# Feed-forward sums: six additions on GpSimd before four TensorE products, and the normalisation on ScalarE

## The chip, the core and the metric

One core of a Trainium2 chip runs the whole program. The engines named here are TensorE (PE in the rows; its weight loads are PEld), VectorE (DVE), ScalarE (ACT), GpSimd (POOL) and the queue that issues DMAs (SP). The metric is the device time of one execution in microseconds. The kernel before takes 1882.07 us, the median of three runs (1881.39 to 1882.36).

## The reference

A transformer block over `x` of 4 x 2048 tokens with 256 channels:

```python
xn = _layernorm(x)
x = x + attention(xn) + ffn(xn)

def ffn(x):                       # W_fc 1024 x 256, W_proj 256 x 1024, both made ternary
    h = jnp.einsum('btd,hd->bth', x, absmean(W_fc))
    h = jax.nn.gelu(h, approximate=False)
    h = layernorm(h, ln_w, ln_b)  # over the 1024 hidden channels
    return jnp.einsum('bth,dh->btd', h, absmean(W_proj))
```

The layernorm inside the feed-forward needs, for each token, the sum of the 1024 values of `gelu(h)` and the sum of their squares. The attention part (16 heads of 16 channels, causal, 2048 tokens) is left as it is by this change.

## The kernel before

The program has three stages with a barrier of all engines between them. The weights are prepared in the first 41 us. The second stage, `project_and_feed_forward`, runs to about 492 us. Attention takes the rest. The change is in the second stage alone.

That stage goes over 8192 tokens in 16 turns (`ch`) of 512 tokens (`CH`). Each turn normalises 4 tiles of 128 tokens (`SUB`), transposes them, and makes three things: queries and keys (lines 884, 821, 729 to 751), values (916, 843) and the feed-forward with its residual (`R`). Each engine's program is written out by hand as a loop, in a fixed order; semaphores alone tie the engines to one another.

TensorE in a turn: the eight blocks of hidden channels (line 904, `hc` 0 to 7, between them the query and key products), the values, `sum_strips` (line 875), `down_projection` for tiles 0 and 1 (line 866), the transposes of the next turn's tokens (line 859), `down_projection` 2 and 3, and `hidden_means` (line 891). ScalarE takes each hidden block out of PSUM with Gelu into `g[:, hc, 0]` (line 831), writes the high half `gh` in fp16 (834) and the square into `g[:, hc, 1]` (836). VectorE makes the low half `gl` from `g` and `gh` (line 722, `low_g`), and a down projection may start only when all eight `gl` are there (`gl_ready`).

The sums over hidden channels are made by TensorE: `strip` is a matrix with ones, and each of 16 products of 128x32 with 128x512 in fp32 adds one block, or its square, into one of four strips of 32 rows of PSUM. Each fp32 product of this form has two records in the trace, so a turn shows 32. ScalarE copies the strips out (line 825), and `hidden_means` turns them into per-token means. VectorE then reads the means (783, `fst`), subtracts them (785), waits for GpSimd's reciprocal square root (`frs`, line 659), and writes `R` (798) from `ft` and `xc`.

GpSimd in a turn makes `rstd` for the next turn's tokens (659), adds a constant row to the tokens (664, `xc`, 128x1024 in fp32) and makes `frs`. VectorE makes the statistics of the next turn's tokens (693, 697, 700), the shift `nmr` (704) and the normalised tokens `xn` (708).

Of the kernel before, what the change touches and what calls it, by code (L numbers as in the profile page):

```python
# [7 lines left out]
ALU = mybir.AluOpType  # L8
# [3 lines left out]
P = 128  # L12
# [4 lines left out]
HC = HID // P  # L17
# [519 lines left out]
def project_and_feed_forward(nc, io, w, scr):  # L537

    with ExitStack() as ctx:
        def sb(name, shape, dt=fp32):  # L540
            return ctx.enter_context(nc.sbuf_tensor(name, shape, dt))
# [18 lines left out]
        gl = sb("gl", [P, HC, CH], fp16)  # L560
        strips = sb("strips", [P, CH])
        fst = sb("fst", [P, SUB, 2])
        fmm = sb("fmm", [P, SUB])
# [25 lines left out]
        gh_ready = sem("gh_ready")  # L589
        g2_ready = sem("g2_ready")  # L590
        gl_ready = sem("gl_ready")
        strips_summed = sem("strips_summed")
# [7 lines left out]
        hidden_bank = [bank[i] for i in (6, 7)]  # L600
        strip_bank = bank[4]
        block = ctx.enter_context(nc.Block())
# [5 lines left out]
        qk_v = [scr[m].rearrange("a b (h e) t -> a b h e t", e=DH) for m in ("Q", "K")]  # L608
        STORES = 2 * 3 * PARTS

        @block.sync
# [45 lines left out]
        def _(pool):  # L657
# [3 lines left out]
            def add_constant(par, loaded):  # L661
# [3 lines left out]
                                   in1=w["CB"][:, None, :].to_broadcast([P, SUB, C]), op=ALU.add).then_inc(xc_ready, 1)  # L665

            add_constant(0, 16)
            def body(i2, par, last):
                ch = i2 * 2 + par
                if not last:  # L670
                    pool.wait_ge(stats_ready, ch + 2)
                    rsqrt(rstd, ve).then_inc(rstd_ready, 1)
                pool.wait_ge(R_ready, ch + 1)
                if not last:
                    add_constant(1 - par, i2 * 16 + 16 + 16 * par)
                pool.wait_ge(fvar_ready, ch + 1)
                rsqrt(frs, fve).then_inc(frs_ready, 1)
# [8 lines left out]
        def _(dve):  # L686
            me = Steps(dve, steps, 13)
            spare = dve.alloc_register("spare_of_dve")
# [12 lines left out]

            def normalise(x, count):
                dve.wait_ge(rstd_ready, count)
                me.done(dve.scalar_tensor_tensor(out=nmr[:, :], in0=mv[:, :, 0], scalar=-1.0, in1=rstd[:, :],
                                                 op0=ALU.mult, op1=ALU.mult))
                me.wait()
                for s in range(SUB):
                    i = dve.tensor_scalar(xn[:, s, :], x[:, s, :], rstd[:, s:s + 1], nmr[:, s:s + 1],
                                          ALU.mult, ALU.add)
                i.then_inc(xn_ready, 1)  # L710

# [43 lines left out]
            def body(i2, par, last):  # L755
# [9 lines left out]
                if not last:  # L765
                    dve.wait_ge(xT_in_psum, ch * 2 + 2)
                    normalise(X[1 - par], ch + 2)
                low_g(ch, 5)
# [42 lines left out]
        def _(act):  # L811
# [5 lines left out]
            def high(m, ch):  # L817
# [3 lines left out]
                act.activation(part[2 * m][:, 0, :], bank[2 * m][:, :], ACT.Copy, scale=w["qscale"][:, 0:1]).then_inc(high_ready, 1)  # L821

            def strips_evac(ch):
                act.wait_ge(strips_summed, ch + 1)
                act.activation(strips[:, :], strip_bank[:, :], ACT.Copy).then_inc(strips_ready, 1)

            def body(ch, last):
                for hc in range(HC + 1):
# [12 lines left out]
                for k in range(2):  # L841
                    act.wait_ge(v_ready, ch * 2 + k + 1)
                    act.activation(Vs[:, 2 * k:2 * k + 2, :], hidden_bank[k][:, :].rearrange("p (s c) -> p s c", s=2),
                                   ACT.Copy, scale=w["pall"][:, 2:3]).then_inc(v_read, 1)
                strips_evac(ch)
                if not last:
                    xT_evac(ch + 1)

            with act.Fori(0, NCH - 1) as ch:
                body(ch, False)  # L850
            body(NCH - 1, True)

        @block.tensor
        def _(pe):
# [14 lines left out]
            def sum_strips(ch):  # L869

                pe.wait_ge(g2_ready, ch * HC + HC)
                for k in range(2):
                    for hc in range(HC):
                        q = hc % 4
                        i = pe.matmul(strip_bank[STRIP * q:STRIP * (q + 1), :], lhsT=w["strip"][:, k, :, :].rearrange("p a k -> p (a k)"),
                                      rhs=g[:, hc, k, :], start=hc + 4 * k < 4, stop=hc + 4 * k >= 8, tile_position=(0, STRIP * q))
                i.then_inc(strips_summed, 1)
# [19 lines left out]
            def body(ch, last):  # L897
# [13 lines left out]
                for k in range(2):  # L911
# [6 lines left out]
                    i.then_inc(v_ready, 1)  # L918
                sum_strips(ch)
                pe.wait_ge(gl_ready, ch * HC + HC)  # L920
                down_projection(ch, 0)
                down_projection(ch, 1)
                pe.wait_ge(v_read, ch * 2 + 2)
                pe.wait_ge(strips_ready, ch + 1)
                if not last:
                    transposes(ch + 1)
                down_projection(ch, 2)
                down_projection(ch, 3)
                for s in range(SUB):
                    hidden_means(s)  # L930
# [958 lines left out]
```

## Time and profile before

| | us |
|---|---|
| time, median of three runs | 1882.07 |
| time of the profiled execution | 1882.02 |
| its span, first to last instruction | 1880.3 |
| TensorE busy | 1818.9 |
| VectorE busy | 1671.0 |
| ScalarE busy | 1590.6 |
| GpSimd busy | 535.9 |

The busy times are sums over the whole span, in which the stage of the change is about a quarter. A turn is read from the timelines further down. A row such as `x4` in a timeline merges neighbouring instructions of one line, and its time runs from the first one's start to the last one's end. Instructions of one engine overlap a little at their ends, so what an instruction costs its engine is read from start to start.

### The profile page before, as it was taken

To read this page: it belongs to the slowest core of one execution; us is meant where nothing else is said; L and a number is where in the kernel's file an instruction comes from. 1 tells how busy PE (TensorE), PEld (TensorE's weight loads), DVE (VectorE), ACT (ScalarE), POOL (GpSimd) and SP (SyncE) were. 2 spreads that over 40 slices of the span, in tenths; PEclk is the share of its full clock that TensorE was granted. 3 is DMA by queue.
4 is the path that set the end of the run, shared out by engine and by line. 5 is a ranking of instruction groups with operands and counts; after the bars stand their busy time and mean duration, and the time that the engine had idled before them with its cause. 6 is when DMAs were issued, how large, how long until landed. Compare 5 with 4: busy or idle time off the path is not lost.

```text
span 1880.3 us, 41858 instructions
## 1 busy us (share of the span) xinstructions
PE 1818.9 (97%) x13875; PEld 682.6 (36%) x13875; DVE 1671.0 (89%) x4759; ACT 1590.6 (85%) x1924; POOL 535.9 (28%) x647
## 2 busy tenths in 40 slices
PE   5999999999799999999999999999999999999998
PEld 3555555655322323223232322323232322323223
DVE  5899999999899999999999999999999999999962
ACT  4675676676169999999999999999999999999994
POOL 1121121121343141433414142341415234141220
PEclk9999999999779999999999999999999999999999
DMA  5233333235531304042331415133141413314112
GB/s 191 63 105 89 88 102 97 84 101 120 107 74 32 65 17 65 22 73 33 70 63 40 65 45 92 32 75 59 44 65 45 86 37 76 59 44 65 36 49 67
DMA packets 160324, 129.01 MB, mean 69 GB/s; under 512 B 95344, under 2 KB 144752, under 8 KB 159768
## 3 DMA queue, kind: packets, MB, share of 16 engines
q1 hardware_dynamic: 158776, 126.45, 30.9%
q8 instruction: 89, 1.46, 0.3%
q14 instruction: 83, 0.68, 0.1%
q10 hardware_dynamic: 1376, 0.43, 0.1%
HBM read 74.60 MB, written 42.98 MB: 63 GB/s over the span
## 4 chain that ended last, share of the span: by engine, by line
PE 42%; ACT 15%; issue 8%; DVE 5%; DMA 1%; POOL 1%; SPq 1%; ACTq 0%; DVEq 0%; POOLq 0%
PE pv L1754 16%; ACT prob L1532 13%; PE sm L1716 10%; PE st L1739 10%; PE sm L1687 3%; PE st L1726 2%; DVE sm L1615 2%; ACT excess L1525 1%; DVE sm L1603 1%; PE sm L1680 1%; DVE pm L1620 1%; DMA scratch_i<-inverse 1%; DVE pm L1603 1%; DVE pm L1615 1%; ACT Y L1515 0%
## 5 line engine op out<-in xcount | busy, mean ns | idle before, releaser
L1532 ACT ACTIVATE prob<-st 128x1024 f32<-128x1024 f32 x1088 | 1048.3, 1028 | 53.8 <-PE st L1739 43.5
L1754 PE MATMUL pv<-prob,V 128*32 128x512 f32 (+3 forms) x5120 | 586.4, 539 | 0.3 <-ACT Y L1515 0.2
L1603 DVE CUSTOM_DVE_ANT_0 sm<-sm,mask 128x256 f32<-128x256 f32 (+3 forms) x1024 | 473.8, 521 | 32.4 <-PE sm L1716 27.8
L1716 PE MATMUL sm<-K,Q 48*128 48x512 f16 (+3 forms) x2112 | 480.1, 349 | 13.3 <-DVE pm L1603 5.6
L1739 PE MATMUL st<-Q,K 50*128 50x512 f16 (+3 forms) x2560 | 479.2, 352 | 10.2 <-ACT prob L1532 6.2
L1620 DVE TENSOR_REDUCE pm<-sm 128x1 f32<-128x512 f32 x640 | 412.4, 684 | 35.1 <-PE sm L1716 31.7
L1491 POOL TENSOR_SCALAR_AFFINE_SELECT prob<-prob 128x256 f32<-128x256 f32 (+1 forms) x448 | 190.6, 439 | 867.7 <-ACT prob L1532 863.1
L1615 DVE CUSTOM_DVE_ANT_0 sm<-sm,excess 128x512 f32<-128x512 f32 x448 | 301.3, 712 | 18.1 <-PE sm L1716 17.2
L1716 PEld LDWEIGHTS sm<-K,Q 48*128 48x128 f16 x2112 | 152.3, 95 | 328.0 <-DVE pm L1615 114.1
L1739 PEld LDWEIGHTS st<-Q,K 50*128 50x128 f16 x2560 | 126.2, 94 | 363.0 <-ACT prob L1532 265.6
L1525 ACT ACTIVATE excess<-st 128x1024 f32<-128x1024 f32 x218 | 220.5, 1025 | 9.1 <-DVE pm L1620 5.1
L1754 PEld LDWEIGHTS pv<-prob,V 128*32 128x32 f32 x5120 | 107.8, 108 | 172.4 <-issue 152.3
L1603 DVE DVE_READ_ACCUMULATOR2_ANT pm<- 128x1 f32 x1024 | 144.9, 142 | 0.1
L831 ACT ACTIVATE g<-bank 128x512 f32<-128x512 f32 x128 | 76.7, 599 | 55.6 <-PE bank L904 55.6
L722 DVE SCALAR_TENSOR_TENSOR gl<-g,wlnw,gh 128x512 f16<-128x512 f32 x128 | 107.0, 875 | 9.6 <-ACT gh L834 9.0
L866 PE MATMUL bank<-wWP,gh 128*128 128x256 f16 x512 | 113.8, 273 | 0.0
L866 PE MATMUL bank<-wWP,gl 128*128 128x256 f16 x512 | 113.6, 273 | 0.0
L1726 PE MATMUL st<-DK,Q 48*128 48x512 f16 x448 | 98.0, 389 | 3.0 <-POOL DK L1444 2.0
L659 POOL TENSOR_TENSOR frs<-fve,wmhalf 128x4 f32<-128x4 f32 x16 | 16.1, 1008 | 286.6 <-DVE fve L789 286.6
L834 ACT ACTIVATE gh<-g,wlnw 128x512 f16<-128x512 f32 x128 | 93.7, 732 | 0.0
L836 ACT ACTIVATE g<-g 128x512 f32<-128x512 f32 x128 | 81.6, 638 | 0.0
L904 PE MATMUL bank<-wxh,wWF 128*128 128x512 f16 x256 | 77.7, 386 | 0.1
(201 smaller groups left out, 1900.3 us busy)
## 6 DMA issues: line engine op xcount, KB each, us to landing
Q<-scratch_q SPq DMA_DIRECT2D x102, 128.0 KB, 4.3
K<-scratch_k SPq DMA_DIRECT2D x102, 128.0 KB, 7.1
x<-in_x SPq DMA_DIRECT2D x16, 512.0 KB, 4.5
scratch_v<-Rt SPq DMA_DIRECT2D x64, 128.0 KB, 2.0
scratch_r<-Rt SPq DMA_DIRECT2D x16, 512.0 KB, 3.2
V_raw<-scratch_v SPq DMA_DIRECT2D x16, 512.0 KB, 9.5
Yc<-Y SPq DMA_DIRECT2D x124, 64.0 KB
spread<-scratch_i SPq DMA_DIRECT2D x124, 64.0 KB, 2.2
```

The source lines that it names most:

```text
L722: dve.scalar_tensor_tensor(out=gl[:, hc, :], in0=g[:, hc, 0, :], scalar=w["lnw"][:, hc:hc + 1], in1=gh[:, hc, :], op0=ALU.mult, op1=ALU.su ...
L866: pe.matmul(bank[s][:, 0:C], lhsT=x[:, hc, s * P:(s + 1) * P], rhs=w["WP"][:, hc, :], start=hc + k == 0, stop=hc + k == HC)
L1491: pool.affine_select(out=x, in_=x, compare_op=ALU.is_ge, fill=0.0, base=0, pattern=[[0, count], [1, P]], channel_multiplier=-1).then_inc(m ...
L1525: act.activation(excess[((slot + ahead) % SLOTS * NX + k) % EXCESSES][:, :, :], st[number % ST][:, :, :], ACT.Relu)\
L1532: act.activation(prob_of(quad, k)[:, :, :], st[number % ST][:, :, :], ACT.Exp).then_inc(exp_done, 1)
L1603: i = dve.tensor_tensor_reduce(x, x, mask[:, CH - block_width(t, k):], 1.0, -3e38, ALU.add, ALU.max, best(h, t, k))
L1615: dve.tensor_tensor_reduce(bank[:, :], bank[:, :], excess[(slot * NX + r) % EXCESSES][:, h % 2, :], 1.0, -3e38, ALU.add, ALU.max, best(h, ...
L1620: dve.tensor_reduce(out=best(h, t, k), in_=bank[:, :], axis=AX.X, op=ALU.max).then_inc(sm_read, 1)
L1716: i = pe.matmul(dst[:, at:at + width], lhsT=Q[slot][r, h // 2, t * P:(t + 1) * P], rhs=K[slot][r, h // 2, k * CH:k * CH + width], start=Tr ...
L1726: i = pe.matmul(st[number % ST][:, g, :], lhsT=Q[slot][rows[g], h // 2, t * P:(t + 1) * P], rhs=DK[slot][rows[g], h // 2, :], start=True, ...
L1739: i = pe.matmul(st[number % ST][:, a, at:at + width], lhsT=K[slot][r, hp, j * P:(j + 1) * P], rhs=Q[slot][r, hp, (c + 1) * CH - width:(c + ...
L1754: i = pe.matmul(pv[2 * DH * h:2 * DH * (h + 1), CH - width:CH], lhsT=V[quad % VSLOTS][:, j, h, :], rhs=prob_of(quad, u)[:, h % 2, at:at + ...
```

## The change

GpSimd adds up seven of the eight blocks: six additions per turn, each of 128x1024 in fp32, since a block and its square lie next to each other in `g`. The sum is kept in `gsum`. TensorE's sums then need four products instead of sixteen: `gsum` and block 7, plain and squared, each in a strip of its own. They stand behind the third down projection instead of ahead of the first, and write into bank 7 instead of bank 4. The normalised tokens are written by ScalarE (four activations with scale and bias) instead of VectorE, behind the evacuation of the values. VectorE keeps the small `nmr`. ScalarE's loop now holds two turns in its body instead of one, since the tokens lie in two buffers.

```diff
-        strip_bank = bank[4]
+        strip_bank = bank[7]
...
+        ADDS = 6
...
+            def add_inner(ch, n):
+
+                pool.wait_ge(g2_ready, ch * HC + n + 2)
+                if n:
+                    pool.wait_ge(gsum_steps, ch * ADDS + n)
+                first = gsum[:, :, :] if n else g[:, 0, :, :]
+                pool.tensor_tensor(out=gsum[:, :, :], in0=first, in1=g[:, n + 1, :, :], op=ALU.add).then_inc(gsum_steps, 1)
...
             def body(i2, par, last):
                 ch = i2 * 2 + par
+                for n in range(2):
+                    add_inner(ch, n)
                 if not last:
                     pool.wait_ge(stats_ready, ch + 2)
                     rsqrt(rstd, ve).then_inc(rstd_ready, 1)
+                for n in range(2, ADDS):
+                    add_inner(ch, n)
                 pool.wait_ge(R_ready, ch + 1)
...
-            def normalise(x, count):
+            def shift(count):
                 dve.wait_ge(rstd_ready, count)
-                me.done(dve.scalar_tensor_tensor(out=nmr[:, :], in0=mv[:, :, 0], scalar=-1.0, in1=rstd[:, :],
-                                                 op0=ALU.mult, op1=ALU.mult))
-                me.wait()
-                for s in range(SUB):
-                    i = dve.tensor_scalar(xn[:, s, :], x[:, s, :], rstd[:, s:s + 1], nmr[:, s:s + 1],
-                                          ALU.mult, ALU.add)
-                i.then_inc(xn_ready, 1)
+                dve.scalar_tensor_tensor(out=nmr[:, :], in0=mv[:, :, 0], scalar=-1.0, in1=rstd[:, :],
+                                         op0=ALU.mult, op1=ALU.mult).then_inc(nmr_ready, 1)
...
+            def normalise(ch, x):
+
+                act.wait_ge(nmr_ready, ch + 1)
+                for s in range(SUB):
+                    i = act.activation(xn[:, s, :], x[:, s, :], ACT.Identity, bias=nmr[:, s:s + 1], scale=rstd[:, s:s + 1])
+                i.then_inc(xn_ready, 1)
...
+                if not last:
+                    normalise(ch, X[1 - par])
+                    xT_evac(ch + 1)
                 strips_evac(ch)
-                if not last:
-                    xT_evac(ch + 1)
...
                 pe.wait_ge(g2_ready, ch * HC + HC)
+                pe.wait_ge(gsum_steps, ch * ADDS + ADDS)
+                inner = [gsum[:, :, :]] + [g[:, hc, :, :] for hc in range(ADDS + 1, HC)]
                 for k in range(2):
-                    for hc in range(HC):
-                        q = hc % 4
+                    for n, x in enumerate(inner):
+                        q = 2 * k + n
                         i = pe.matmul(strip_bank[STRIP * q:STRIP * (q + 1), :], lhsT=w["strip"][:, k, :, :].rearrange("p a k -> p (a k)"),
-                                      rhs=g[:, hc, k, :], start=hc + 4 * k < 4, stop=hc + 4 * k >= 8, tile_position=(0, STRIP * q))
+                                      rhs=x[:, k, :], start=True, stop=True, tile_position=(0, STRIP * q))
...
-                sum_strips(ch)
                 pe.wait_ge(gl_ready, ch * HC + HC)
                 down_projection(ch, 0)
                 down_projection(ch, 1)
                 pe.wait_ge(v_read, ch * 2 + 2)
-                pe.wait_ge(strips_ready, ch + 1)
                 if not last:
                     transposes(ch + 1)
                 down_projection(ch, 2)
+                sum_strips(ch)
                 down_projection(ch, 3)
+                pe.wait_ge(strips_ready, ch + 1)
```

GpSimd's program of one turn before, in the loop; L659 is the reciprocal square root, L664 the constant row:

```order
L659 TENSOR_TENSOR rstd<-ve,wmhalf 128x4 [waits stats_ready]
L673 REGISTER_ALU
L663 ISA [waits R_ready]
L664 TENSOR_TENSOR xc<-x,wCB 128x1024 [waits x_loaded1]
L659 TENSOR_TENSOR frs<-fve,wmhalf 128x4 [waits fvar_ready]
```

The same turn now, from its second addition on; L677 is the addition, L663 the reciprocal square root, L668 the constant row:

```order
L677 TENSOR_TENSOR gsum<-gsum,g 128x1024 [waits gsum_steps]
L685 REGISTER_ALU
L663 TENSOR_TENSOR rstd<-ve,wmhalf 128x4 [waits stats_ready]
L673 REGISTER_ALU
L675 REGISTER_ALU [waits g2_ready]
L677 TENSOR_TENSOR gsum<-gsum,g 128x1024 [waits gsum_steps]
L673 REGISTER_ALU
L675 REGISTER_ALU [waits g2_ready]
L677 TENSOR_TENSOR gsum<-gsum,g 128x1024 [waits gsum_steps]
```

Two additions stand ahead of `rstd` and four behind it, ahead of `xc` and `frs`.

TensorE's program before, where the values end and the down projection begins (L916 values, L875 strips, L866 down projection):

```order
L916 MATMUL bank<-wWVl,wxh 128x256
L916 MATMUL bank<-wWVh,wxl 128x256
L875 MATMUL bank<-g,wstrip 32x512 [waits g2_ready]
L875 MATMUL bank<-g,wstrip 32x512 x15
L866 MATMUL bank<-wWP,gh 128x256 [waits qk_read,gl_ready]
L866 MATMUL bank<-wWP,gl 128x256
```

And now the place between the third and the fourth down projection (L887), where the strips (L898) stand:

```order
L887 MATMUL bank<-wWP,gh 128x256
L887 MATMUL bank<-wWP,gl 128x256
L893 ISA [waits g2_ready]
L898 MATMUL bank<-gsum,wstrip 32x512 [waits gsum_steps]
L898 MATMUL bank<-g,wstrip 32x512
L898 MATMUL bank<-gsum,wstrip 32x512
L898 MATMUL bank<-g,wstrip 32x512
L887 MATMUL bank<-wWP,gh 128x256 [waits qk_read]
```

Directly behind the values now comes the first down projection, which waits for `gl_ready`.

## Rows read from the trace of the kernel before

**Rows 1.** Stretches: length, busy us by engine, granted clock, DMA share, GB/s

```profile
152.00:180.00 28.00, 27.82 (x196) 16.20 (x194) 25.85 (x54) 18.41 (x32) 5.15 (x3) 1.00 0.33 94
180.00:208.00 28.00, 27.82 (x196) 16.22 (x194) 25.80 (x54) 18.41 (x32) 4.62 (x3) 1.00 0.33 94
```

**Rows 2.** Timeline of TensorE: start us, us, operation, [idle before]

```profile
169.21 3.64 PE L875 MATMUL bank<-g,wstrip 128*32 128x512 f32 x32
172.79 0.28 PE L866 MATMUL bank<-wWP,gh 128*128 128x256 f16 x1
...
176.29 1.04 PE L859 MATMUL bank<-ident,xn 128*128 128x128 f32 x8
...
180.66 0.95 PE L891 MATMUL bank<-wmean_cols,strips 128*128 128x2 f32 x8
181.47 0.59 PE L904 MATMUL bank<-wxh,wWF 128*128 128x512 f16 x2
```

**Rows 3.** Timeline of VectorE, the same turn, from one `fst` copy to the next

```profile
181.42 0.15 DVE L783 COPY fst<-bank 128x2 f32<-128x2 f32 x1
...
185.24 0.23 DVE L792 TENSOR_SCALAR frw<-frs,wwmax 128x4 f32<-128x4 f32 x1 [1.12 <-POOL frs L659]
185.76 1.67 DVE L798 SCALAR_TENSOR_TENSOR Rt<-ft,frw,xc 128x256 f32<-128x256 f32 x4 [0.29 <-DVE frw L792]
187.35 1.41 DVE L722 SCALAR_TENSOR_TENSOR gl<-g,wlnw,gh 128x512 f16<-128x512 f32 x2
188.67 1.40 DVE L693 BATCH_NORM_STATS2 st<-x 128x6 f32<-128x256 f32 x4
...
190.81 4.19 DVE L722 SCALAR_TENSOR_TENSOR gl<-g,wlnw,gh 128x512 f16<-128x512 f32 x3
...
195.11 1.38 DVE L708 TENSOR_SCALAR xn<-x,rstd,nmr 128x256 f32<-128x256 f32 x4
...
199.05 0.75 DVE L735 SCALAR_TENSOR_TENSOR rope<-bank,wqscale,wcos 128x512 f32<-128x512 f32 x1
...
204.78 1.51 DVE L739 SCALAR_TENSOR_TENSOR rot<-bank,wqscale,wsin 64x512 f32<-64x512 f32 x2
...
209.32 0.15 DVE L783 COPY fst<-bank 128x2 f32<-128x2 f32 x1
```

**Rows 4.** Timeline of GpSimd, the same turn

```profile
190.84 1.02 POOL L659 TENSOR_TENSOR rstd<-ve,wmhalf 128x4 f32<-128x4 f32 x1 [5.63 <-DVE ve L700]
191.82 2.63 POOL L664 TENSOR_TENSOR xc<-x,wCB 128x1024 f32<-128x1024 f32 x1
```

**Rows 5.** Line 664 on GpSimd: ns min/median/max, first and last start

```profile
L664 POOL TENSOR_TENSOR xc<-x,wCB x16: 2338/2660/2873, 40.4 to 443.2; 128x1024 f32<-128x1024 f32 x16
```

**Rows 6.** Line 722 on VectorE, as above

```profile
L722 DVE SCALAR_TENSOR_TENSOR gl<-g,wlnw,gh x128: 737/747/2847, 45.5 to 474.4; 128x512 f16<-128x512 f32 x128
```

**Rows 7.** Line 704 on VectorE, as above

```profile
L704 DVE SCALAR_TENSOR_TENSOR nmr<-mv,rstd x15: 148/151/2355, 54.3 to 443.6; 128x4 f32<-128x4 f32 x15
```

**Rows 8.** Groups of VectorE, 506.4 to 508.8 us: count, busy us, mean ns

```profile
L1603 DVE CUSTOM_DVE_ANT_0 sm<-sm,mask 128x256 f32<-128x256 f32 x4 | 1.6, 441 | 0.0
```

**Rows 9.** Timeline of GpSimd in the same stretch

```profile
506.44 2.34 POOL L1436 TENSOR_TENSOR apart<-apart 128x1024 f32<-128x1024 f32 x1
```

**Rows 10.** Timeline of ScalarE, second square, evacuations of V

```profile
186.11 0.62 ACT L836 ACTIVATE g<-g 128x512 f32<-128x512 f32 x1
...
196.95 1.29 ACT L843 ACTIVATE Rt<-bank,wpall 128x512 f32<-128x512 f32 x2
```

**Rows 11.** Stretches around the end of the stage and the recovery of the clock

```profile
487.00:491.00 4.00, 0.00 (x0) 0.00 (x0) 2.63 (x11) 0.00 (x0) 1.02 (x1) 0.99 0.63 148
491.00:495.00 4.00, 1.55 (x8) 0.95 (x8) 2.07 (x8) 0.00 (x0) 1.82 (x4) 0.50 0.38 131
...
542.00:547.00 5.00, 5.00 (x49) 1.60 (x49) 4.46 (x13) 4.58 (x6) 0.64 (x1) 0.99 0.02 5
```

**Rows 12.** Stretch at the start of the stage

```profile
41.00:43.74 2.74, 2.69 (x7) 1.03 (x8) 0.00 (x0) 1.42 (x2) 1.75 (x1) 0.50 0.00 0
```

More of the change, by code:

```diff
@@ L561, in project_and_feed_forward @@
         strips = sb("strips", [P, CH])
+        gsum = sb("gsum", [P, 2, CH])
         fst = sb("fst", [P, SUB, 2])
@@ L590, in project_and_feed_forward @@
         g2_ready = sem("g2_ready")
+        gsum_steps = sem("gsum_steps")
+        nmr_ready = sem("nmr_ready")
         gl_ready = sem("gl_ready")
@@ L686, in _ @@
         def _(dve):
-            me = Steps(dve, steps, 13)
+            me = Steps(dve, steps, 12)
             spare = dve.alloc_register("spare_of_dve")
@@ L766, in body @@
                     dve.wait_ge(xT_in_psum, ch * 2 + 2)
-                    normalise(X[1 - par], ch + 2)
+                    shift(ch + 2)
                 low_g(ch, 5)
@@ L825, in strips_evac, with body @@
                 act.activation(strips[:, :], strip_bank[:, :], ACT.Copy).then_inc(strips_ready, 1)
-            def body(ch, last):
+            def body(ch, par, last):
                 for hc in range(HC + 1):
@@ L844, in body @@
                                    ACT.Copy, scale=w["pall"][:, 2:3]).then_inc(v_read, 1)
+                if not last:
+                    normalise(ch, X[1 - par])
+                    xT_evac(ch + 1)
                 strips_evac(ch)
-                if not last:
-                    xT_evac(ch + 1)
-            with act.Fori(0, NCH - 1) as ch:
-                body(ch, False)
-            body(NCH - 1, True)
+            with act.Fori(0, NCH // 2 - 1) as i2:
+                for par in range(2):
+                    body(i2 * 2 + par, par, False)
+            for par in range(2):
+                body(NCH - 2 + par, par, par == 1)
         @block.tensor
```

## The prediction

> **What bounds the kernel now.** I read the stretches first, since the busy shares of the whole span mix three stages. In a steady turn of the feed-forward stage TensorE is busy 27.82 of 28 us and VectorE 25.8, ScalarE 18.4 and GpSimd 5 [rows 1]. Two engines are candidates, so I read both timelines for the length of a turn. TensorE goes from the first hidden product at 181.47 back to the strips at 169.21 without a gap that it could close [rows 2]; its turn is 27.82 us. VectorE goes from one `fst` copy at 181.42 to the next at 209.32, so 27.90 us [rows 3], and in between its only wait of note is the 1.12 us for GpSimd's `frs` plus 0.29. Both engines are full, VectorE by a hair the slower. Taking work off TensorE alone can therefore gain nothing; the sum has to be made on VectorE.
>
> The second thing to see is in what VectorE's 25.8 us consist of. Three `gl` instructions took 4.19 us, while two took 1.41 (start to start 1.32, so 0.66 each) [rows 3]. Three should take 2.07, so 2.1 us are lost. At that moment GpSimd ran its only long instruction, `xc`, for 2.63 us [rows 4]. It is not chance: of 128 `gl` the median is 747 ns and the longest 2847 [rows 6], of 15 `nmr` the median is 151 ns and the longest 2355 [rows 7], and `xc` itself is 2338 ns alone and 2660 in the median [rows 5]. So a VectorE instruction with both inputs in SBUF (`g` and `gh`, `mv` and `rstd`) and a GpSimd addition that reads SBUF exclude each other: whichever asks second waits for the other's whole reading. VectorE lost 2.1 of 2.34 us, so I count 2.15 per collision, and GpSimd 0.3 to 0.5. Instructions that read PSUM and one SBUF tile are not held: four 128x256 ones took 0.44 us each on average beside a GpSimd addition of 2.34 us [rows 8, 9].
>
> **The change, part by part.**
>
> TensorE: 32 records of strips in 3.58 us (169.21 to 172.79) become 8 in 0.9 [rows 2]; its turn alone would be 27.82 - 3.58 + 0.9 = 25.1 us. The later place costs nothing in itself: the strips' evacuation (0.65 us, half of line 843's 1.29 [rows 10]) lies beside the fourth down projection (1.75 us, half of 172.79 to 176.29). But the 3.58 us had stood between the values and the first down projection, which waits for the eighth `gl`; that cover is gone, and `gl` decides at once.
>
> ScalarE: four activations of 128x256 replace VectorE's normalisation. Their form is not in the trace; they are at least nothing and at most the two evacuations of 128x512 twice over, 2 x 1.29 us [rows 10]. ScalarE has 9 us idle per turn [rows 1] and TensorE needs `xn` only behind two down projections, so I take 1.3 and count it as nothing on the path. If VectorE were so late that `nmr` came after the values' evacuation, `xn` would follow some 1.5 us behind `nmr`, which is still before the first down projection. One table load in two turns goes as well, behind the evacuations where ScalarE is idle. SP's load of `x` waits for an `xn` of the turn before, and is not late.
>
> VectorE: the normalisation goes, 1.38 us, start to start some 1.35. VectorE's turn without any collision: 27.9 - 2.1 - 1.35 = 24.4 us.
>
> GpSimd: six additions of the size of `xc`. Alone 6 x 2.34 = 14 us; GpSimd would have 5 + 14 = 19 busy of 28, which looks free. It isn't, because of the collisions. I walk one turn from the rows, counted from the first hidden product (181.47 is 0):
> - `R` runs from 4.3 to 5.9, two `gl` would follow to 7.2. The second square ends at 5.3 (186.11 + 0.62) [rows 10]. The first addition asks at 5.3, gets in behind an `R`, and holds the next VectorE instruction 2.15 us.
> - The second addition asks while the first `gl` runs, gets in behind it, and holds the second `gl` 2.15 us. Statistics end at 13.3, `rstd` (1.02 us) at 14.5.
> - The third gets in behind the next two `gl` and holds the third, the fourth is behind that and holds `nmr` or the `gl` after it, the fifth holds a `gl` for 1.5 to 2.15 (0.66 of it may lie beside the `part` instruction, which reads PSUM), the sixth holds the eighth `gl` 2.15 us. It ends near 26.
> - `xc` then lies beside `rope` and `rot`, which read PSUM, or holds one more instruction.
>
> That makes 5.7 to 7 collisions per turn in place of one: 12.2 to 15 us. I take six, 12.9 us, since the two ends are close: VectorE's turn is 24.4 + 12.9 = 37.3 us.
>
> TensorE against that: the values end at 15.6, the first down projection starts with the eighth `gl` near 26, a gap of 10 us in every turn. Behind it VectorE needs 7.24 us to the end of the second `rot` (199.05 to 206.29) [rows 3], then come the fourth down projection and the means, 1.75 + 0.81: the next turn begins 9.8 us behind the eighth `gl`, near 36 to 38. The gap has a second price. At the stage's end TensorE idled from 487 us on; the granted clock was 0.99 up to 491 and 0.50 after it [rows 11], that is 1.2 instead of 2.4 GHz. At the start of the stage it was 0.50 for the first 2.7 us of products and full after [rows 12]. A few us at half clock in the down projections cost 1.6, of which the wait for `rot` hides part. I add 0.5: the turn is 37.8 us, 9.9 more than before (27.85, the mean of the two engines).
>
> The whole: 14 middle turns x 9.9 = 139 us. The first turn starts with an empty VectorE, which waits for its first `gl` anyway: about +5. The last has six additions and no `xc`, statistics or normalisation; four collisions on the path, +8. Together +152 us. Attention is untouched behind its barrier. The profiled execution took 1882.02 us (span 1880.3 and 1.7 around it), 0.05 from the median, so the time is 1882 + 152 = **2034 us**.
>
> **The rivals.**
>
> A. *The additions hide.* GpSimd gets in only where VectorE reads PSUM, and nothing is held. Then TensorE's 25.1 us bound the turn (VectorE 24.4), -2.7 x 16 = -43: 1839 us; with the one old collision kept, VectorE's 26.5 and 1860 us. For it: much of VectorE's turn reads PSUM or one SBUF tile, and those instructions are not held [rows 8]. Against it: in each of the two forms of turn the one long GpSimd instruction of the stage hit a VectorE instruction for its full length [rows 6, 7]. 10%.
>
> B. *VectorE keeps the ports while it has work in a row.* A held addition waits until VectorE issues something else, so each run of two-input instructions is hit at most once: `R` with two `gl`, three `gl` with `nmr` and a fourth, the last two `gl`, one of the two fp16 splits. 24.4 + 4 x 2.15 = 33.0, +5.15 x 15 = +77: 1960 us. Against it: in [rows 3] the addition got in between the second and the third of three `gl` in a row. 15%.
>
> The Trainium skill (SBUF — State Buffer, section "Who interferes with whom") says that issue order, not the shape of the operation, decides who blocks, and that the loser waits for the whole instruction. By that rule it is the forecast's walk and 2034 us, not B; the third `gl` of that row agrees with it.
>
> C. *TensorE's clock stays low.* At the start of attention it stayed at half from 491 to 542 us though TensorE was busy again. If the gap of 10 us leaves it at half for 7 to 12 us of each turn, the down projections and the strips double (their 8 us lie behind the eighth `gl`) and outlast `rot`: a turn of 39.5 to 41.5, +185 to +215 us, 2065 to 2095. Against it: at the stage's start it was back within 3 us [rows 12]. 14%.
>
> D. *Seven full collisions* is within the forecast: 39.5 us per turn, 2060. That the change does nothing to the time (the additions run, nobody waits for them and nobody gains) needs A and a VectorE that stays at 27.9: 2%.
>
> **How the numbers follow.** Forecast 59% (its own range 2005 to 2065), A 10%, B 15%, C 14%, no change 2%. The range from 1952 to 2085 holds the forecast, B and half of C. What this measurement can tell from no change is 0.2%, 3.8 us. Faster is A alone: 0.10; same 0.02; all else is slower: 0.88.
>
> **What would show it.** In the new profile `gl` should have a mean near 1.9 us, with its long ones near 2.85; the additions should take 2.6 to 3.0 us instead of 2.34; TensorE should show about 10 us idle per turn ahead of line 887, ended by `gl`; and the strips' 8 records should take 0.9 us without a wait for `gsum`. The first hidden products should lie 37 to 39 us apart. If instead `gl` stays near 0.7 us and TensorE runs without a gap, A is right. If additions take far over 3 us and TensorE waits for `gsum` at line 898, it is B. If the granted clock of a whole turn is under 0.8, it is C. I am wrong altogether if the stage ends before 492 us.

## The result, and the profile after

The changed kernel took 2004.35 us (median of four runs, 2004.25 to 2005.48) against 1882.09 for the kernel before (four runs, 1881.39 to 1882.36). The ratio is 1.0649, with a 95% interval from 1.0636 to 1.0663: slower by 122 us. The prediction was 2034 us.

First the page of the changed kernel: busy time, the granted clock by slices, and the groups that the change touches.

```profile
PE 1813.8 (91%) x13491; PEld 686.6 (34%) x13491; DVE 1799.5 (90%) x4699; ACT 1611.5 (80%) x1976; POOL 787.5 (39%) x743
...
PEclk8988898898886899999999999999999999999999
...
L887 PE MATMUL bank<-wWP,gh 128*128 128x256 f16 x512 | 148.2, 322 | 128.6 <-DVE gl L733 128.6
...
L677 POOL TENSOR_TENSOR gsum<-gsum,g 128x1024 f32<-128x1024 f32 x80 | 213.8, 2672 | 5.7
L733 DVE SCALAR_TENSOR_TENSOR gl<-g,wlnw,gh 128x512 f16<-128x512 f32 x128 | 197.3, 1582 | 6.3 <-ACT gh L852 6.3
```

The row of `gl` in the page of the kernel before:

```profile
L722 DVE SCALAR_TENSOR_TENSOR gl<-g,wlnw,gh 128x512 f16<-128x512 f32 x128 | 107.0, 875 | 9.6 <-ACT gh L834 9.0
```

TensorE waits 128.6 us in all ahead of the down projections, and each time for `gl`; `gl` itself has a mean of 1582 ns, where its mean before was 875. That is the whole result in two rows, but it does not yet say who holds `gl`, nor that nothing else is longer. Next, tile by tile (ns min/median/max, first and last start):

```profile
L733 DVE SCALAR_TENSOR_TENSOR gl<-g,wlnw,gh x128: 734/752/2858, 46.3 to 599.9; 128x512 f16<-128x512 f32 x128
L720 DVE SCALAR_TENSOR_TENSOR nmr<-mv,rstd x15: 2297/2305/2342, 55.2 to 556.2; 128x4 f32<-128x4 f32 x15
L677 POOL TENSOR_TENSOR gsum<-gsum,g x80: 2354/2679/2815, 51.0 to 595.5; 128x1024 f32<-128x1024 f32 x80
L668 POOL TENSOR_TENSOR xc<-x,wCB x16: 2331/2338/2343, 40.8 to 566.9; 128x1024 f32<-128x1024 f32 x16
L838 ACT ACTIVATE xn<-x,nmr,rstd x60: 583/586/644, 59.8 to 560.1; 128x256 f32<-128x256 f32 x60
```

Of `gl` the median is still near that of before (752 ns, 747 before [rows 6]), so a part of them is held and the others are not: of the 128, 41 take about 2.83 us, 15 about 2.17 and the rest about 0.75. `nmr`, which works on 128x4 elements, is now held every time; before it was the exception [rows 7]. `xc` is no longer slowed (2338 ns, [rows 5]).

The stretches (first row: one turn, from its first hidden product to the next turn's; second row: the turn after it; then the gap of the first of them, and two parts of what lies behind that gap; columns as in [rows 1]):

```profile
218.07:254.65 36.58, 27.86 (x171) 16.55 (x171) 34.20 (x52) 20.49 (x36) 20.69 (x9) 0.86 0.26 74
254.65:289.70 35.05, 26.98 (x170) 16.08 (x170) 32.96 (x48) 19.21 (x35) 20.71 (x9) 0.90 0.26 73
233.00:242.00 9.00, 0.70 (x7) 0.39 (x4) 9.00 (x7) 3.92 (x8) 8.77 (x5) 0.74 0.11 29
242.00:247.00 5.00, 4.76 (x23) 3.39 (x24) 4.94 (x6) 0.00 (x0) 4.69 (x2) 0.50 0.00 0
247.00:254.00 7.00, 7.00 (x62) 5.36 (x60) 6.62 (x11) 2.86 (x4) 0.00 (x0) 0.95 0.24 74
```

In the first of the two turns VectorE is busy for 34.2 of 36.6 us, TensorE for 27.9. In the gap VectorE and GpSimd are both full, and behind the gap the clock is at 0.50, which is the lower of its two levels, 1.2 GHz. Turns of 36.6 and 35.0 us alternate; the mean of the fourteen middle ones is 35.81, where it was 27.83.

The two timelines of that turn show who holds whom. VectorE:

```profile
218.19 0.15 DVE L794 COPY fst<-bank 128x2 f32<-128x2 f32 x1
...
222.54 3.78 DVE L809 SCALAR_TENSOR_TENSOR Rt<-ft,frw,xc 128x256 f32<-128x256 f32 x4 [0.29 <-DVE frw L803]
226.25 3.51 DVE L733 SCALAR_TENSOR_TENSOR gl<-g,wlnw,gh 128x512 f16<-128x512 f32 x2
...
231.69 2.08 DVE L733 SCALAR_TENSOR_TENSOR gl<-g,wlnw,gh 128x512 f16<-128x512 f32 x3
233.68 2.33 DVE L720 SCALAR_TENSOR_TENSOR nmr<-mv,rstd 128x4 f32<-128x4 f32 x1
...
237.26 4.92 DVE L733 SCALAR_TENSOR_TENSOR gl<-g,wlnw,gh 128x512 f16<-128x512 f32 x2
242.10 0.74 DVE L746 SCALAR_TENSOR_TENSOR rope<-bank,wqscale,wcos 128x512 f32<-128x512 f32 x1
...
245.07 2.17 DVE L758 TENSOR_TENSOR rope<-rope,rot 128x512 f32<-128x512 f32 x1
...
252.07 0.68 DVE L758 TENSOR_TENSOR rope<-rope,rot 128x512 f32<-128x512 f32 x1
...
254.15 0.16 DVE L794 COPY fst<-bank 128x2 f32<-128x2 f32 x1 [0.22 <-PE bank L914]
```

And GpSimd:

```profile
223.41 2.63 POOL L677 TENSOR_TENSOR gsum<-g 128x1024 f32<-128x1024 f32 x1 [1.42 <-ACT g L854]
226.12 2.43 POOL L677 TENSOR_TENSOR gsum<-gsum,g 128x1024 f32<-128x1024 f32 x1
231.84 1.47 POOL L663 TENSOR_TENSOR rstd<-ve,wmhalf 128x4 f32<-128x4 f32 x1 [3.29 <-DVE ve L716]
233.28 11.10 POOL L677 TENSOR_TENSOR gsum<-gsum,g 128x1024 f32<-128x1024 f32 x4
244.35 2.33 POOL L668 TENSOR_TENSOR xc<-x,wCB 128x1024 f32<-128x1024 f32 x1
```

Lay one over the other and each long VectorE row has its addition: `R` took 3.78 instead of 1.67 (+2.11), the first two `gl` 3.51 instead of 1.41 (+2.10), `nmr` 2.33 instead of 0.15 (+2.18), the last two `gl` 4.92 instead of 1.41 (+3.51, two additions), the sum of `rope` and `rot` 2.17 instead of the 0.68 of its twin at 252.07 (+1.49, held by `xc`). Together 11.4 us. Three `gl` with no addition beside them took 2.08. The prediction had VectorE's turn without collisions at 24.4 us, and 24.4 + 11.4 = 35.8. VectorE's own turn, from the `fst` copy at 218.19 to that at 254.15, is 35.96 us with 0.22 of waiting for TensorE in it. The mean of the fourteen turns is 35.8 as well. In the turn after it the first two additions hold the first two `gl` (5.62 us for the two) instead of `R` and one `gl`, and the sum of the holds is again 11.4.

The last rows that matter are what ended TensorE's gap, and ScalarE's normalisation:

```profile
236.05 2.07 ACT L838 ACTIVATE xn<-x,nmr,rstd 128x256 f32<-128x256 f32 x4 [1.20 <-DVE nmr L720]
...
242.24 0.40 PE L887 MATMUL bank<-wWP,gh 128*128 128x256 f16 x1 [8.54 <-DVE gl L733]
```

`xn` was ready at 238.1 and TensorE used it at 248.37. The 0.40 us of the first product, against 0.28 before [rows 2], is the half clock.

Over the whole: the fourteen middle turns cost 14 x 7.98 = 112 us more, the first turn 4.4 (33.58 after 29.14), the last 8.9 (41.1 after 32.3). That is 125; attention took 1384.0 instead of 1387.2 us, which leaves 122. The code of attention is the same in all kernels here, and it took between 1383.7 and 1387.2 us in their eleven profiles, so 3 us there say nothing of the change.

### The profile page after: what moved, and what is told of

It is laid out like the page before. It is cut to its first block, busy times and chain, and to the rows that moved or that the text cites. A ratio compares the mean times of both kernels' runs of the same rounds, so it can differ in the third digit from the quotient of the medians.

```text
span 2002.5 us, 41290 instructions
## 1 busy us (share of the span) xinstructions
PE 1813.8 (91%) x13491; PEld 686.6 (34%) x13491; DVE 1799.5 (90%) x4699; ACT 1611.5 (80%) x1976; POOL 787.5 (39%) x743
## 4 chain that ended last, share of the span: by engine, by line
PE 42%; ACT 13%; issue 7%; DVE 5%; DMA 1%; SPq 1%; POOL 1%; ACTq 0%; DVEq 0%; POOLq 0%
PE pv L1777 16%; ACT prob L1555 11%; PE sm L1739 10%; PE st L1762 10%; PE sm L1710 3%; PE st L1749 2%; DVE sm L1638 2%; ACT excess L1548 1%; DVE sm L1626 1%; DVE pm L1643 1%; DMA scratch_i<-inverse 1%; PE sm L1703 1%; DVE pm L1638 1%; DVE pm L1626 0%; PE sm L1734 0%
## 5 line engine op out<-in xcount | busy, mean ns | idle before, releaser
L887 PE MATMUL bank<-wWP,gh 128*128 128x256 f16 x512 | 148.2, 322 | 128.6 <-DVE gl L733 128.6
L677 POOL TENSOR_TENSOR gsum<-gsum,g 128x1024 f32<-128x1024 f32 x80 | 213.8, 2672 | 5.7
L733 DVE SCALAR_TENSOR_TENSOR gl<-g,wlnw,gh 128x512 f16<-128x512 f32 x128 | 197.3, 1582 | 6.3 <-ACT gh L852 6.3
L887 PE MATMUL bank<-wWP,gl 128*128 128x256 f16 x512 | 146.8, 320 | 0.0
L826 ACT ACTIVATE wxh<-bank 128x512 f16<-128x512 f32 x30 | 16.3, 595 | 153.6 <-PE bank L880 153.6
L887 PEld LDWEIGHTS bank<-wWP,gh 128*128 128x128 f16 x512 | 58.9, 115 | 160.6 <-DVE gl L733 133.0
```

Of the source, the lines that this page charges most:

```text
L677: pool.tensor_tensor(out=gsum[:, :, :], in0=first, in1=g[:, n + 1, :, :], op=ALU.add).then_inc(gsum_steps, 1)
L733: dve.scalar_tensor_tensor(out=gl[:, hc, :], in0=g[:, hc, 0, :], scalar=w["lnw"][:, hc:hc + 1], in1=gh[:, hc, :], op0=ALU.mult, op1=ALU.su ...
L887: pe.matmul(bank[s][:, 0:C], lhsT=x[:, hc, s * P:(s + 1) * P], rhs=w["WP"][:, hc, :], start=hc + k == 0, stop=hc + k == HC)
```

## The experiments

The theory after the result: an addition that reads SBUF on GpSimd and a VectorE instruction with two SBUF inputs cannot run side by side, so that the second waits for the first, and the turn is the sum of VectorE's work and these holds. The rivals: TensorE's lowered clock behind the gap sets the turn (the prediction's C), or the rearrangement itself costs (the strips no longer cover the wait for `gl`). Ratios are against the kernel before on the same chip, with 95% intervals.

### No additions, the strips in their new place

```diff
-                for n in range(2):
-                    add_inner(ch, n)
...
-                for n in range(2, ADDS):
-                    add_inner(ch, n)
...
-                pe.wait_ge(gsum_steps, ch * ADDS + ADDS)
-                inner = [gsum[:, :, :]] + [g[:, hc, :, :] for hc in range(ADDS + 1, HC)]
+                inner = [g[:, hc, :, :] for hc in range(HC)]
```

TensorE makes sixteen products again, in rounds over the four strips.

> The changed kernel without the six additions; TensorE makes all sixteen products, in the new place behind the third down projection, and ScalarE still normalises. Collision theory: only xc is left to hold VectorE, whose turn is 24.4 + 2.1 = 26.5 us, and TensorE's own 27.8 us bound it again, with 0.3 to 0.6 us of waiting for the eighth gl now that the strips no longer stand ahead of it: 1882 to 1892 us. Rival (the new place of the strips, or the normalisation on ScalarE whose four activations take 2.07 us, delays the turn): it stays well over 1920 us, near 2004 if they are the whole cause.

Measured: 1890.68 us, ratio 1.0043 [1.0026, 1.006]; a steady turn is 28.61 us. The changed order with the normalisation on ScalarE costs 8 us; the other 114 are the additions'. Waits of TensorE and VectorE in the stage (us in total, times, longest):

```profile
PE bank L883 <- DVE rot L746: 3.8, 14, 0.3
PE bank L883 <- DVE gl L729: 2.3, 14, 0.2
```

TensorE, still with all sixteen products, now meets `gl` and `rot` a little early in every turn: it waits 0.17 + 0.27 us. Counted from the start of one product to the start of the next, otherwise 0.11 us, the two places take 0.44 (200.77 to 201.21) and 0.54 (202.86 to 203.40), so 0.33 + 0.43 more; that is the 0.78 us by which the turn is longer than before. It is the loss of the cover of which the prediction spoke, with its price when `xc` alone holds VectorE (in the median `nmr` takes 2322 ns here).

### Writes of the same size in place of the additions

```diff
-                first = gsum[:, :, :] if n else g[:, 0, :, :]
-                pool.tensor_tensor(out=gsum[:, :, :], in0=first, in1=g[:, n + 1, :, :], op=ALU.add).then_inc(gsum_steps, 1)
+                pool.tensor_tensor(out=pad4[:, :], in0=w["mhalf"][:, :], in1=w["mhalf"][:, :], op=ALU.add)
+                for k in range(2):
+                    i = pool.memset(gsum[:, k, :], 1.0)
+                i.then_inc(gsum_steps, 1)
```

This kernel leaves the hidden sums out. Each addition becomes one of 128x4 and two writes of 128x512.

> Each of the six additions is replaced by a tiny addition of 128x4 (which carries the wait) and two memsets of 128x512 into gsum, so GpSimd is busy at the same places in its order and TensorE waits for it in the same way, but it hardly reads SBUF (the hidden sums are left out of the computation). Collision theory (what is held is the reading): gl and R run at their 0.75 and 0.48 us except beside xc; VectorE's turn is 24.4 + 2.1 = 26.5 us, TensorE's 25.2 with a wait for gl: 1858 to 1870 us. Rival (any GpSimd instruction of some length holds VectorE, or the order of waits is what costs): over 1900 us, with gl held by the length of the memsets.

Measured: 1846.21 us, ratio 0.9803 [0.9788, 0.9818], turn 25.60 us. The two tiles:

```profile
L736 DVE SCALAR_TENSOR_TENSOR gl<-g,wlnw,gh x128: 739/747/753, 46.5 to 441.8; 128x512 f16<-128x512 f32 x128
...
L679 POOL MEMSET gsum<- x192: 518/522/531, 48.8 to 441.9; 128x512 f32 x192
```

192 writes of 128x512 stood at the same places of GpSimd's program, and of 128 `gl` none was longer than 753 ns. The writes are shorter than the additions (0.52 us each, two for one addition of 2.34), but a `gl` held by one for its length would have shown over 1 us. So it is GpSimd's reading that holds VectorE, not that GpSimd is busy, nor its writing. The Trainium skill (SBUF — State Buffer, section "Who interferes with whom") says the same, that a GpSimd instruction which only writes does not contend with a VectorE instruction that has two SBUF inputs; this row agrees. The time itself, 37 us under the kernel before, is what the fewer products on TensorE would give if the additions held nobody. It is 12 us below the bottom of what I had expected, since `xc` had moved: it held only the `rope` sum, for 0.34 us (1.02 instead of 0.68), where I had counted 2.1.

### Three additions, begun where they stand

```diff
-        ADDS = 6
+        ADDS = 3
```

TensorE makes ten products, over the same four strips.

> The changed kernel with three additions instead of six (ten products on TensorE), at the places where the first three stood. Collision theory: four collisions per turn (three additions and xc) instead of six, 24.4 + 7.9 = 32.3 us per turn: 1940 to 1955 us. Rival (the cost is one fixed wait, not proportional to the number): near 2004. Second rival (TensorE's half clock in the gap is a good part of the cost): under 1930.

Measured: 1999.51 us, ratio 1.0622 [1.0605, 1.064]. **This missed by 45 us and more**: half of the additions gone, and 5 us won. Collisions were counted rightly: three additions and `xc` hold the first `gl`, the second, `nmr` and the sixth `gl`. VectorE, at 24.4 + 4 x 2.1 = 32.8 us, should have given turns of 33. The stretches of one turn (up to the values' end, the gap, behind the gap), and two waits of the stage:

```profile
254.70:270.17 15.47, 15.29 (x82) 7.17 (x81) 13.76 (x29) 14.14 (x26) 8.44 (x5) 1.00 0.39 102
270.17:276.87 6.70, 0.17 (x2) 0.00 (x1) 6.70 (x6) 3.39 (x7) 4.12 (x2) 0.74 0.00 0
276.87:289.98 13.11, 13.11 (x100) 9.29 (x101) 10.28 (x17) 1.68 (x3) 0.00 (x0) 0.87 0.25 75
```

```profile
PE bank L887 <- DVE gl L733: 90.8, 14, 6.6
...
DVE fst L794 <- PE bank L916: 39.3, 14, 3.2
```

VectorE now waits 2.8 us per turn for the means. The path is no longer VectorE all through: it is VectorE up to the eighth `gl`, where all four holds lie, and from there TensorE without a pause, 13.1 us of products at a mean clock of 0.87. A hold ahead of the eighth `gl` is paid in full, and the idle time that it makes on TensorE is paid again in clock. It called for the two runs that follow.

### Idle products in the gap, with three additions and with six

```diff
                     i.then_inc(v_ready, 1)
+                for _ in range(26):
+                    pe.matmul(bank[4][:, :], lhsT=w["WF"][:, 0, 0:P], rhs=xh[:, 0, :], start=True, stop=True)
                 pe.wait_ge(gl_ready, ch * HC + HC)
```

The products' result is not used. With six additions there are 36 of them.

> The same with the three additions as they stood: 26 idle products (5.6 us) in the gap of 6.5 us. In that kernel VectorE was idle 2.4 to 3.1 us per turn and TensorE's part behind the eighth gl took 13.1 us at mixed clock instead of 10.9. Clock theory: the turn falls from 35.8 to 33.2 to 33.6 us, 1960 to 1968 us. Rival (the clock is not what held it; the wait for rot or the strips is): no change, 1996 to 2001 us.

> The changed kernel with 36 idle products of 128x512 in fp16 (7.8 us) between the values and the wait for the eighth gl, into a bank that is free there, so that TensorE isn't idle for 8.6 us. VectorE-bound theory: the granted clock stays at 1.00, the down projections take 3.5 us for two, and the turn is still VectorE's 35.6 us: 1996 to 2004 us. Rival (the half clock is part of the turn): a turn of 35 us or less, under 1992 us.

Measured with three: 1975.62 us, ratio 1.05 [1.0484, 1.0516], turn 34.13 in most (mean 34.03). Waits of the stage:

```profile
DVE fst L794 <- PE bank L916: 19.7, 15, 2.5
...
PE bank L887 <- DVE gl L733: 11.9, 14, 1.0
```

24 us are won by work that does nothing: with TensorE busy through the gap the stretch behind `gl` shrinks from 13.1 to 12.0 us and VectorE's wait for the means to 1.2. So the half clock stood on the path there. It is 8 us short of what I had expected: the stretch behind `gl` still lasts 12.0 us, 2.7 of them the strips with ten products, 0.27 a wait for `rot`.

Measured with six: 2003.75 us, ratio 1.0644 [1.0628, 1.066], turn 35.67, mean clock 0.984 instead of 0.95. The interval overlaps that of the changed kernel (1.0636 to 1.0663), so the times cannot be told apart; the profiled turn is 0.14 us shorter. For there VectorE decides behind the gap as well: `xc` holds the `rope` sum, and in the changed kernel `fst` waits for TensorE in five turns only, 0.3 us at the longest. Theory C named a real cost that the changed kernel hardly pays.

### Three additions, placed

GpSimd's body: the first addition behind the second `gl`, the second behind the eighth, the third behind the first `part` sum, and `xc` behind TensorE's first means.

```diff
-        ADDS = 6
+        ADDS = 3
...
-                for n in range(2):
-                    add_inner(ch, n)
+                pool.wait_ge(gl_ready, ch * HC + 2)
+                add_inner(ch, 0)
...
-                for n in range(2, ADDS):
-                    add_inner(ch, n)
+                pool.wait_ge(gl_ready, ch * HC + HC)
+                add_inner(ch, 1)
+                pool.wait_ge(part_ready, ch * 2 + 1)
+                add_inner(ch, 2)
...
+                    pool.wait_ge(ffn_ready, ch * 4 + 1)
```

> The same three additions, but each is started by a semaphore where VectorE reads PSUM or one SBUF tile: the first behind the second gl (beside the statistics), the second behind the eighth gl (beside rope and rot), the third behind the first fp16 split (beside the second rope and rot); xc starts with the means. Collision theory with the place deciding: hardly any VectorE instruction is held, VectorE's turn is about 25 us and TensorE's 27.8 - 6/16 of 3.6 = 26.5 us bounds it: 1858 to 1868 us. Rival (the number of GpSimd instructions decides, not the place): 1940 to 1955 us, as with the three where they stood.

Measured: 1883.47 us, ratio 1.0006 [0.9996, 1.0015], turn 27.98. Against the same number of additions at their old places that is 116 us less. In the steady turns no instruction with two SBUF inputs is held (`gl` median 744 ns, additions 2349 to 2366), so the placement, of the additions and of `xc`, and not the amount, makes the cost. But the time missed the expected one by 15 us. TensorE's wait ahead of the strips says why:

```profile
PE bank L903 <- POOL gsum L677: 8.4, 14, 0.6
```

The third addition comes late for the strips. And the ten products took 2.7 us, as long as twelve do: four strips work side by side, and ten products are three rounds, as twelve are. The third addition bought nothing and cost a wait.

### Two additions, placed

```diff
-        ADDS = 3
+        ADDS = 2
...
-                pool.wait_ge(part_ready, ch * 2 + 1)
-                add_inner(ch, 2)
```

The edit is shown against the version with three. TensorE makes twelve products.

> Two placed additions instead of three. Three of them left ten products, which four strips take in three rounds (2.7 us, the same as twelve), and TensorE waited 0.6 to 0.9 us for the third addition. With two there are twelve products, the same three rounds, and no wait: TensorE's turn is 27.8 - 0.9 + 0.2 = 27.1 to 27.2 us: 1869 to 1874 us. Rival (the waits for rot and the longer tail behind gl bound the turn, whatever the strips do): 1881 to 1885, like three placed.

Measured: 1872.31 us, ratio 0.9943 [0.9929, 0.9957]: faster than both kernels, 11 us under before. In the profiles the stage ends at 485.4 us instead of 493.1, so 8 of the 11 are the stage's and the rest lies within the spread of attention. The stretch of one turn, and GpSimd's timeline in it:

```profile
206.50:233.81 27.31, 26.96 (x186) 15.71 (x186) 22.94 (x50) 19.07 (x35) 9.53 (x5) 1.00 0.34 96
```

```profile
206.53 2.35 POOL L668 TENSOR_TENSOR xc<-x,wCB 128x1024 f32<-128x1024 f32 x1 [9.03 <-PE bank L917]
209.19 1.02 POOL L663 TENSOR_TENSOR frs<-fve,wmhalf 128x4 f32<-128x4 f32 x1 [0.30 <-DVE fve L801]
213.84 2.35 POOL L677 TENSOR_TENSOR gsum<-g 128x1024 f32<-128x1024 f32 x1 [3.64 <-ACT g L855]
216.30 1.44 POOL L663 TENSOR_TENSOR rstd<-ve,wmhalf 128x4 f32<-128x4 f32 x1
222.44 2.36 POOL L677 TENSOR_TENSOR gsum<-gsum,g 128x1024 f32<-128x1024 f32 x1 [4.70 <-DVE gl L734]
```

The additions lie beside the statistics (one SBUF input) and beside `rope` and `rot` (PSUM), `xc` beside the `ft` rows (PSUM). Each takes 2.35 us, its time alone, and VectorE is busy 22.9 us. TensorE is the bound, 26.96 of 27.31 us at full clock.

One instruction with a single SBUF input is held all the same, `ve`, a TENSOR_SCALAR of 128x4 in the tail of the first addition (213.84 to 216.19). First here, then in the kernel with six additions, where none lies beside it but once:

```profile
L717 DVE TENSOR_SCALAR ve<-mv x15: 629/632/636, 50.4 to 434.1; 128x4 f32<-128x4 f32 x15
```

```profile
L716 DVE TENSOR_SCALAR ve<-mv x15: 169/170/410, 50.5 to 554.2; 128x4 f32<-128x4 f32 x15
```

It loses 0.46 us, fifteen times of fifteen, while the BATCH_NORM_STATS2 rows beside the same addition take their usual 1.40 us for four. The turn does not feel it, since VectorE has 1.2 us to spare.

### Two additions, placed, the normalisation back on VectorE

```diff
-                    i = act.activation(xn[:, s, :], x[:, s, :], ACT.Identity, bias=nmr[:, s:s + 1], scale=rstd[:, s:s + 1])
...
+                    i = dve.tensor_scalar(xn[:, s, :], x[:, s, :], rstd[:, s:s + 1], nmr[:, s:s + 1],
+                                          ALU.mult, ALU.add)
```

> Two placed additions, and the normalisation back on VectorE. Theory (with xc and the additions out of its way VectorE has room for 1.35 us more, of which the waits for gh take up about 1): the eighth gl comes 0.3 to 0.4 us later, the turn is 27.5 instead of 27.3 us, 1872 to 1878 us. Rival (the move to ScalarE is what makes the placed version gain): 1.35 us per turn more, 1890 us and over.

Measured: 1877.02 us, ratio 0.9972 [0.9961, 0.9982]. The interval does not touch that of the version above, and the times are 5 us apart. But the move to ScalarE is worth only about 2 of them: the turns are 27.45 us against 27.31, and the stage ends 2.0 us later (487.4 against 485.4). The other 2.7 us of the two profiles lie in attention, which the edit does not touch. VectorE has 1.2 us idle per turn ahead of `fst` in both.

### Four additions, placed

```diff
-        ADDS = 2
+        ADDS = 4
...
+                pool.wait_ge(gl_ready, ch * HC + 6)
+                add_inner(ch, 1)
                 pool.wait_ge(gl_ready, ch * HC + HC)
-                add_inner(ch, 1)
+                add_inner(ch, 2)
+                add_inner(ch, 3)
```

The edit is shown against the version with two and the normalisation on ScalarE. TensorE makes eight products.

> Four additions, of which three lie beside reads of PSUM as far as that goes: behind the second gl, behind the sixth gl, behind the eighth gl, and the last directly behind it; eight products in two rounds. Collision theory: the second addition holds the seventh gl for about 1.3 us, the fourth holds the addition of rope and rot for 1.9 us, which makes the second rot late for the fourth down projection: 27.2 to 27.6 us per turn, 1870 to 1878 us, no gain over two additions. Rival (two rounds fewer on TensorE decide): 26.2 us per turn, near 1856.

Measured: 1913.67 us, ratio 1.0163 [1.0149, 1.0177]. **Missed by 36 us and more.** I had expected that the two rounds saved would just pay for the collisions; they did not come near it. VectorE's timeline:

```profile
204.47 3.21 DVE L737 SCALAR_TENSOR_TENSOR gl<-g,wlnw,gh 128x512 f16<-128x512 f32 x2
...
210.57 2.68 DVE L762 TENSOR_TENSOR rope<-rope,rot 128x512 f32<-128x512 f32 x1
...
219.26 2.81 DVE L766 TENSOR_TENSOR part<-rope,part 128x512 f16<-128x512 f32 x1
221.99 0.15 DVE L798 COPY fst<-bank 128x2 f32<-128x2 f32 x1
```

The second addition, at 204.12, found two `gl` (3.21 instead of 1.41); the pair behind the eighth `gl` was too long for the PSUM rows and held the `rope` sum (2.68); and `xc`, which starts with the means at 219.17, found VectorE late by then and held the split that should have been over (2.81 instead of 0.69). Most turns are 28 or 31 us long, one after the other (mean 29.9, extremes 27.7 and 32.4). My reading, which no run isolates, is that a hold late in one turn shifts where the next turn's additions fall. The strips did what was hoped, eight products in 1.9 us. Whether four additions find free places with another order of VectorE's instructions was not tried.

## Why the prediction was right, and where it was off

The measured 2004.35 us lie inside the stated outer range, and 0.65 us below the forecast's own range, whose lower end was 2005.

- **Both engines are full, so VectorE makes the sum.** Right. 24.4 us without collisions plus 11.4 measured is the measured turn of 35.8.
- **The collision at 2.1 us.** Right: 2.11, 2.10, 2.18 where the hold was whole. That it is the reading, which [rows 8, 9] could only suggest, was shown by the run with writes. The sentence that instructions reading one SBUF tile are not held is too wide: `ve`, a TENSOR_SCALAR, was held wherever an addition lay beside it.
- **How many.** The term was mis-sized: 12.9 us (six at 2.15, 12.2 at the least) forecast, 11.4 measured. Six instructions are held, as counted, but two of them for less: four for 2.1 us, the seventh `gl` for 1.43 and the `rope` sum for 1.49. That the number six is right is in part luck. The walk had the sixth addition hold the eighth `gl` and `xc` lie free beside `rope`. In fact the third addition held `nmr`, the fourth the seventh `gl`, the fifth the eighth (3.51 us for the two), the sixth addition started at about 241.7 beside `rope` and `rot` and held nobody, and `xc` behind it came onto the sum of `rope` and `rot`, which reads two SBUF tiles, for 1.49.
- **The gap and its clock.** The gap is 8.54 us in that turn (10 forecast), ended by `gl`. The half clock came as feared; the means of the clock over a turn (0.90 and 0.86) make it 7 or 10 us of each, in the longer turn some 4.7 of them in the gap itself (0.74 over 9 us). But it cost at most about 0.14 us per turn, not 0.5, since VectorE is late too. With the collisions this makes the turn 8.0 us longer where 9.9 were forecast: 14 x 1.9 = 27 of the 30 us by which the number was too high.
- **First and last turn.** +5 and +8 forecast, +4.4 and +8.9 measured. The second is right in size only: all six additions held a `gl` in the last turn, not four (16.64 us for six `gl`, 12.6 more than they need), and 2.8 us of that took the place of waits for ScalarE that VectorE had there before.
- **TensorE's strips** took 1.0 us for 8 records (0.9 forecast), with no wait for `gsum`. Right.
- **Normalisation on ScalarE.** 4 x 586 ns in 2.07 us, where I took 1.3; the range went to 2.58, and it lies 10 us ahead of its use. Right that it does not count.
- **A, the additions hide.** Excluded as placed here, yet it is what the placed versions do: there `gl` stays at 0.74. The writes show what it would be worth, 1846 us; A's 1839 was close.
- **B, one hold per run of instructions.** Excluded: two additions hit two `gl` in a row (4.92 us), 2.08 and 1.43.
- **C, a low clock.** Shown as a real mechanism and as hardly this kernel's: 24 us with three additions, under 1 and within the noise with six. Its 2065 us for a turn of 39.5 counted sixteen such turns; by the forecast's own sum (fourteen, +5 and +8) it would have been 2058.
- **The signs named ahead.** The additions' 2.68 us, the strips and TensorE's wait for `gl` came as said. The wait was 8.0 us per turn and not 10, the mean of `gl` 1.58 us and not 1.9, the turns 35.0 and 36.6 us and not 37 to 39, all on the side of fewer and shorter holds.

## What to carry to other kernels

Before an elementwise sum goes to an idle GpSimd, list VectorE's instructions of that stretch by their inputs: the sum costs VectorE its full reading time (here 2.1 us for 128x1024) beside each instruction with two SBUF inputs, and nothing beside those that read PSUM, or beside BATCH_NORM_STATS2 with its single tile. A TENSOR_SCALAR with a single tile is not free (0.46 us here, all that was left of the addition). So make GpSimd wait for the place, and count the places before the additions. A hold ahead of the instruction that a full TensorE waits for may be paid twice, in the gap and in the clock behind it. And if products run side by side in four strips, their number matters only in rounds of four.

## What the runs showed of the hardware that was not expected

- A hold does not depend on how small VectorE's instruction is: `nmr`, 128x4, was held 2.3 us fifteen times of fifteen. GpSimd's own 128x4 instruction did not hold: `rstd` ran from 231.84 for 1.47 us beside three `gl`, which took 2.08.
- A VectorE instruction with one SBUF input can be held too: `ve`, TENSOR_SCALAR of 128x4, took 0.63 us instead of 0.17 in all fifteen turns of the version with two placed additions, and ended with the addition.
- Both sides take turns. While VectorE and GpSimd each have work in a row, one instruction of each passes at a time: four additions in 11.10 us instead of 9.4, and one VectorE instruction with two SBUF inputs between any two of them.
- fp32 products of 128x32 by 512 columns, four side by side: 1.0 us for four products, 1.9 for eight, 2.7 for ten and for twelve, 3.6 for sixteen [rows 2] (the profile shows each product as two records).
- Turns of two lengths alternate although the program is the same in each: 36.6 and 35.0 us between TensorE's first hidden products, with half clock for about 10 and 7. VectorE's `fst` copies lie 36.0 and 35.6 us apart in the same two turns, so most of the alternation is TensorE starting a turn earlier or later than VectorE needs it; behind the gap TensorE takes 12.4 us in the long turn (242.24 to 254.65) and 11.5 in the short one (278.17 to 289.70). What carries the difference from one turn to the next was not settled.
